# A language-model tower on one core: items of the front pipeline moved by a unit

## The reference

```python
logits = flat_x @ router_w + router_b
top_vals, top_idx = jax.lax.top_k(logits, K)      # K = 2 of E = 8 experts
rw = jax.nn.softmax(top_vals, axis=1)
def step(carry, xt):
    h, c = carry
    gates = xt @ Wi + h @ Wh + b
    i_, f_, g_, o_ = jnp.split(gates, 4, axis=-1)
    c = jax.nn.sigmoid(f_) * c + jax.nn.sigmoid(i_) * jnp.tanh(g_)
    h = jax.nn.sigmoid(o_) * jnp.tanh(c)
    return ((h, c), h @ Wo + bo)
```

## Time and profile before

| | us |
|---|---|
| median of three runs | 1628.14 |
| lowest and highest | 1626.41, 1628.58 |
| the profiled execution's own time | 1628.72 |
| its span, first to last instruction | 1626.9 |
| busy: TensorE, VectorE, ScalarE, POOL | 1549.8, 1491.1, 859.5, 58.1 |
| prologue, until step 0's first tanh | 101.4 |
| step 0 | 51.9 |
| a steady step (559.0 to 660.1) | 101.1 |
| step 14, step 15 | 93.8, 63.8 |

### The profile page before, as it was taken

The page is one execution under the profiler, slowest core; times in us unless marked ns, Lnnn a source line. Parts: engine busy times, 40 slices in busy tenths (PEclk is TensorE's granted clock), DMA queues, the critical chain, the costliest instruction groups (busy, mean ns, idle before and its releaser), DMA issues.

```text
span 1626.9 us, 21424 instructions
## 1 busy us (share of the span) xinstructions
PE 1549.8 (95%) x7325; PEld 742.2 (46%) x7325; DVE 1491.1 (92%) x2442; ACT 859.5 (53%) x1022; POOL 58.1 (4%) x47
## 2 busy tenths in 40 slices
PE   7778999999999999999999999999999999999998
PEld 3433444444444444454444444444444444444543
DVE  4777999999999999999999999999999999999986
ACT  4445455455554555555565464654646546465554
POOL 1000000000000000000000000000000000000000
PEclk8989999999999999999999999999999999999999
DMA  3325435444454543645435454464544535445453
GB/s 94 88 57 151 144 116 153 148 126 145 118 160 136 128 143 123 157 139 139 137 126 146 139 140 139 124 146 135 144 136 128 151 125 153 130 130 149 125 148 90
DMA packets 252545, 215.65 MB, mean 133 GB/s; under 512 B 131175, under 2 KB 174147, under 8 KB 252437
## 3 DMA queue, kind: packets, MB, share of 16 engines
q1 hardware_dynamic: 252356, 214.27, 46.9%
q10 hardware_dynamic: 80, 0.02, 0.0%
HBM read 73.17 MB, written 4.74 MB: 48 GB/s over the span
## 4 chain that ended last, share of the span: by engine, by line
DVE 61%; issue 16%; PE 13%; ACT 6%; POOL 2%; DMA 1%; SPq 1%; DVEq 0%; ACTq 0%
DVE H L1169 8%; DVE tmp L1202 8%; DVE C L1176 6%; DVE C L1206 5%; DVE tmp L1194 5%; DVE xm L1161 4%; PE gates L653 3%; PE gates L650 3%; DVE H L1184 3%; DVE z L1215 2%; POOL rstd L1301 2%; PE gates L655 2%; DVE xn L968 1%; DVE stats L935 1%; PE yp L661 1%
## 5 line engine op out<-in xcount | busy, mean ns | idle before, releaser
L819 ACT ACTIVATE tmp<-gates,bias_sb 128x1024 f32<-128x1024 f32 (+1 forms) x504 | 533.7, 1062 | 407.5 <-PE gates L655 373.3
L653 PE MATMUL gates<-H,wh_sb 128*128 128x512 f32 x960 | 491.9, 594 | 0.0
L655 PE MATMUL gates<-H,wh_sb 128*128 128x512 f32 x896 | 458.5, 593 | 0.0
L650 PE MATMUL gates<-xm,wi_sb 128*128 128x512 f16 x1512 | 413.3, 383 | 22.9 <-ACT tmp L819 17.4
L650 PEld LDWEIGHTS gates<-xm,wi_sb 128*128 128x128 f16 x1512 | 142.1, 99 | 315.9 <-issue 192.6
L655 PEld LDWEIGHTS gates<-H,wh_sb 128*128 128x128 f32 x896 | 170.8, 191 | 215.4 <-issue 215.4
L826 ACT ACTIVATE tmp<-C 128x1024 f32<-128x1024 f32 (+1 forms) x128 | 128.5, 1004 | 253.4 <-DVE C L1206 246.8
L653 PEld LDWEIGHTS gates<-H,wh_sb 128*128 128x128 f32 x960 | 182.9, 191 | 69.5 <-issue 0.5
L1194 DVE SCALAR_TENSOR_TENSOR tmp<-tmp 128x1024 f32<-128x1024 f32 (+1 forms) x120 | 140.8, 1174 | 17.9 <-ACT tmp L819 17.9
L1176 DVE COPY_PREDICATED C<-masks,Cx 128x1024 f32<-128x1024 uint16 (+1 forms) x120 | 154.3, 1286 | 0.0
L1184 DVE SCALAR_TENSOR_TENSOR H<-tmp 128x1024 f32<-128x1024 f32 (+1 forms) x128 | 147.7, 1154 | 5.3 <-ACT tmp L826 4.9
(11 more groups left out here) (286 smaller groups left out, 1238.8 us busy)
## 6 DMA issues: line engine op xcount, KB each, us to landing
Hx<-H SPq DMA_DIRECT2D x232, 256.0 KB, 2.9
Cx<-C SPq DMA_DIRECT2D x232, 256.0 KB, 2.4
masks<-mask_scratch SPq DMA_DIRECT2D x128, 256.0 KB, 5.1
roww<-mw_scratch SPq DMA_DIRECT2D x128, 256.0 KB, 3.4
diag<-pr SPq DMA_DIRECT2D x60, 112.0 KB, 3.5
diag<-vwin SPq DMA_DIRECT2D x60, 112.0 KB, 3.2
out_dram<-h SPq DMA_DIRECT2D x16, 256.0 KB, 2.6
C<-in_wi SPq DMA_DIRECT2D x1, 2048.0 KB, 10.8
```

Source lines behind the costliest of these rows:

```text
L650: last = mm(fed, wi_sb[:, e, wpart, rows_of], xm[:, e % 2, vpart, :], start=(wpart == HI and vpart == HI), stop=(first and wpart == LO))
L653: last = mm(fed, wh_sb[:, e, rows_of], H[:, e, 0:SEQ], start=False, stop=True)
L655: last = mm(other, wh_sb[:, e, rows_of], H[:, e, SEQ:2 * SEQ], start=True, stop=True)
L819: A(tmp[:, gate_at(gate, e), 0:width(s)], gates[:, (n - 1) % 2, 0:width(s)], ACT.Tanh, bias=bias_sb[:, e, gate:gate + 1], scale=UNSCALE).t ...
```

## The change

Items move in the four tables; nothing is computed differently. ScalarE's copies after `qkv` are cut into `q` (unit 27) and `kv` (unit 28), and `split` goes to unit 29. `moments` goes from unit 23 to 22 and the embedding's items from 22 to 21. `pw` goes behind `q_lo`, `kv_lo` from unit 29 to 30; `v_win`, `summary`, `window`, the feature part, `proj`, `projT`, `x2T`, `moments2`, `xn2`, `choice` and `weights` go one unit on, `f_part` two. `add_y` goes from unit 7 to 6, in front of the cell. `EARLY` becomes 17. In step 0 `chosen` stands a unit sooner, ahead of the input part.

```diff
-    SP_AT = dict(ids=-16, qbd=-3, vz=1, rows=25, wrow=28)
-    PE_AT = dict(emb=-10, xT=-6, qkv=-5, summary=-2, window=0, feature=6, values=12, proj=15, projT=16, x2T=19,
+    SP_AT = dict(ids=-17, qbd=-2, vz=1, rows=25, wrow=28)
+    PE_AT = dict(emb=-11, xT=-6, qkv=-5, summary=-1, window=1, feature=7, values=12, proj=16, projT=17, x2T=20,
                  logits=21, maskT=25)
-    ACT_AT = dict(h=-10, xT=-6, qkv=-5, split=-4, summary=0, window=3, pr_hi=7, feature=8, proj=15, x2T=19,
-                  choice=21, maskT=25)
-    DVE_AT = dict(onehot=-14, moments=-9, xn=-8, pw=-4, q_lo=-4, kv_lo=-3, v_win=-2, w_max=-1, s_max=1, s_sub=2, w_sum=3,
-                  w_out=4, s_sum=5, s_norm=6, f_max=7, p_lo=8, p_T=9, f_sum=10, f_part=10, attn=13,
-                  moments2=16, xn2=17, x_lo=20, choice1=21, choice2=21, weights=22)
-    EARLY = 16
+    ACT_AT = dict(h=-11, xT=-6, q=-5, kv=-4, split=-3, summary=0, window=4, pr_hi=8, feature=9, proj=16, x2T=20,
+                  choice=22, maskT=25)
+    DVE_AT = dict(onehot=-15, moments=-10, xn=-8, pw=-3, q_lo=-4, kv_lo=-2, v_win=-1, w_max=0, s_max=2, s_sub=3, w_sum=4,
+                  w_out=5, s_sum=6, s_norm=7, f_max=8, p_lo=9, p_T=10, f_sum=11, f_part=12, attn=13,
+                  moments2=17, xn2=18, x_lo=21, choice1=22, choice2=22, weights=23)
+    EARLY = 17
...
-    YT_AT, YBACK_AT, YADD_AT = 5, 6, 7
+    YT_AT, YBACK_AT, YADD_AT = 5, 6, 6
...
-                if t == ACT_AT["qkv"]:
+                if t == ACT_AT["q"]:
...
                     last.then_inc(S["qhi"], 1)
+                if t == ACT_AT["kv"]:
                     act.wait_ge(S["kp"], b1)
...
-                    if t == YADD_AT and not first:
-                        add_y(s - 1, 1 - par)
...
-                    if g == 2 and e:
+                    if first and g == 1 and e:
                         chosen(s, e - 1)
-                    elif g == 2 and not first:
+                    if g == 2 and e and not first:
+                        chosen(s, e - 1)
+                    elif g == 2 and not e and not first:
                         chosen(s - 1, E - 1)
                     run_front(lambda u, b: front(u, b, b % 2), t, s)
                     if g == 1:
                         input_part(s, e, first)
+                    if t == YADD_AT and not first:
+                        add_y(s - 1, 1 - par)
                     if g == 2 and not first:
                         cell(s, e)
```

## The result

The change makes the kernel slower: 1653.32 us median (1649.02 to 1653.85) against 1628.14 (1625.42 to 1628.58), a ratio of 1.0146 [1.0135, 1.0158]. Forecast were 1622.5 us and 1611 to 1636. The profiled execution took 1653.85 us, its span is 1652.1, 25.2 us over that of before.

| us | before | after | difference | forecast |
|---|---|---|---|---|
| prologue | 101.4 | 106.4 | +5.0 | |
| step 0 | 52.0 | 55.8 | +3.8 | both together -0.5 |
| steps 1 to 13 | 1315.9 | 1332.4 | +16.5 | -5.2 |
| steps 14, 15 | 157.7 | 157.4 | -0.2 | 0 |

The account below looks back on a forecast made before the run. It took a once-per-step loop through nearly full VectorE and TensorE as the bound: 0.40 us less per step, -5.2 over 13, and -0.5 in prologue and step 0, gave 1622.5 us, range 1611 to 1636.

Parts of the forecast that it names:

- piece A: VectorE alone, from unit 29's input part to the start of swap_c at unit 27: 93.36 us before, 93.67 forecast after.
- Rival (5): POOL's power beside the cell holds VectorE up, 1.9 - 0.4 us per step, 1642 us in all; chance 0.03.
- TensorE's waits "cost nothing": New waits at values (0.1 us), y of unit 16 (0.5) and projT (0.9) cost nothing; VectorE has over 0.8 in hand.
- piece B: Rest of the step's loop, swap_c of unit 27 to unit 29's input part: 7.69 us before, 6.98 forecast, decided by TensorE.
- one batch of the prologue: One batch of 13 idle matmuls (2.97 us) goes; clock effect taken as 0, at the other end +3 us.
- the block copies: First operand blocks (qbd), issued by SP at unit 30: about 6 us needed, over 11 available, so no cost.
- The gain of moments: Moments a unit sooner: VectorE's 0.90 us wait for POOL's power ahead of xn leaves each step.
- the price of kv_lo: kv_lo moves to unit 30 and adds 1.21 us per step to VectorE's own stretch of the loop.
- the relief of ScalarE: The split copies move behind tanh 29, taking 1.06 us per step out of ScalarE's stretch of the loop.
- no wait at unit 1, unit 2 or for masks: Input part 1 and cell 2 taken at nothing (ends 0 and 0.5 us per step); masks with 1 us to spare.
- y_bias free: add_y ahead of cell frees y_bias of its 0.5 us wait and delays cell by 0.6, neither in the loop.
- Rival (3): Gain replaced: 0.4 us per step at input part 1 or cell 2, or prologue's 3.5 not returned; 1628 us, chance 0.20.

## Why the prediction was wrong, point by point

The forecast's span was 1626.9 - 5.7 = 1621.2 us, the measured one is 1652.1: 30.9 us too few. The runs split them (differences of spans by stage):

| us | |
|---|---|
| steps 1 to 13 without low clock: 1315.2 by the run with idle matmuls, forecast 1310.7 | +4.5 |
| low clock in them: 1332.4 - 1315.2 | +17.2 |
| prologue and step 0: 162.2, forecast 152.9 | +9.3 |
| steps 14 and 15 | -0.2 |

**The step that failed** is one sentence: the other moves "(summary, window and feature parts one unit on, f_part two, moments2, xn2, choice and weights one) stay inside A and change only its order, at nothing, if each input is in time". xn2's input was not in time. The prediction priced the first norm's power at 1.92 us and took the second's, behind moments2, as unchanged (1.39 us before). But that duration depends on what VectorE runs when the power starts. moments2 went to unit 17, and the one-hot rows came to the same unit from 18. The diff shows it in `onehot=-15`, and neither the list of moved items nor the prediction names it. The price is read from the run with the input part first, whose units are all those of the changed kernel: piece A is 93.1 us there and 94.1 here (steps with full clock), 1.0 us per step. That the forecast's 93.67 is only 0.4 off is luck: without the wait piece A is 0.55 us shorter than the forecast's sum, and no run isolates what saves that.

**Rival (5) had the right two engines and the wrong loser.** It let POOL hold VectorE up beside the cell, and that did not come: L1203 and L1207 took 1.22 and 1.23 us beside the power. VectorE held POOL up, at the other power. The text even used "no more than elsewhere" on VectorE's row alone; that POOL's own power took 1.92 us there and 1.39 at the other norm of the same trace was not asked after. The Trainium skill's "SBUF — State Buffer" (two separate sides) says of the shared ports that the later one fully blocks until the first has finished. The prediction found the trace against this page because hidden kept its 1.23 us. But hidden (635.31) had started ahead of the power (635.48), so by the page's rule POOL is the one to wait. For POOL the traces agree where VectorE's instruction, with two inputs in SBUF, is already running. The power takes 1.01 us beside an idle VectorE, and 1.39, 1.91 and 1.92 where an instruction ends 0.5 or 1.0 us after its start, each over about 0.9 us after that end. The page's rule does not give 2.9 or 4.7 us, through several instructions. Nor does it give that VectorE goes on at once with its next instruction at its usual duration, as swap_h does in before (612.93, 1.30 us) beside the rest of the power.

**TensorE's waits "cost nothing"** was the second failed step, and the dearest. In the loop alone it is right: with full clock piece B is 6.96 us against 6.98 forecast, with maskT waiting 0.30 (forecast 0.5) and projT 0.72 (0.9). But the wait of 1.30 us at the logits, which the prediction did not work out, has half clock behind it in eight of the twelve steps 2 to 13, and with it piece B of 8.2 to 8.6 us and in three steps a cell at unit 22 that waits over 1 us. With that wait filled by idle matmuls the half clock is gone and 17.2 us with it. The Trainium skill's "TensorE: Matmul & The Clock Gate" (Part 1) has half clock after idling; the forecast weighed it for one batch of the prologue only. The traces agree in that half clock follows a wait, but not every wait brings it.

**Prologue and step 0.** The forecast said for the block copies "go out at unit 30, need about 6 us and have over 11", which holds in the steps. In the prologue the same unit stands behind wh's load on SP. It was not looked at: 12.2 us, 6.0 of them in the prologue and 6.2 behind it in step 0. Without it the two would have been 2.9 us shorter than the forecast's 152.9, within its 4. The 12.2 us are not wh's alone, though: with the norm back, the other order of SP gave 6.3 (batch included), and with wh's load where it is, the norm back or the one-hot rows back shortened step 0 by 5.4 and 4.4 us. The causes share part of step 0. The idle matmuls that were lost are 11 and not 13: the table's entry of 13 took the place of the 11 at unit 21, and unit 22 has none (7314 matmuls in all against 7325).

**What held.** The gain of moments, 0.90 forecast and 0.86 measured per step (11.2 us over steps 1 to 13); the price of kv_lo and the relief of ScalarE, alone 1.31 (94.74 less a mean of 93.43 before) and 1.05 against 1.21 and 1.06; waits ahead of q_lo, pw and the input part at 0.81, 0.42 and 1.23 in the undisturbed step (0.9, 0.5, about 1); no wait at unit 1, unit 2 or for masks; y_bias free. Rival (3), the gain replaced by a stall, came true in the steps with full clock (101.0 us, as before), at a place that it did not name.

**Open:** why the clock falls behind the logits in some steps and not in others of the same waits, and why it holds with the norm back, where TensorE waits 0.8 and 1.4 us 14 to 20 us ahead of the logits. Shown is only that with the logits' idle time filled no step from 1 to 14 has it. Why step 0 follows wh's load was not tried.

## What to carry to other kernels

Try the parts of a change one at a time: here the embedding's items and moments, moved by themselves, were worth all of the gain (0.9930), and the other parts that were tried nothing or less. Before moving an item, look at the other engine's small instruction that it hands work to: what stands right behind the hand-over is part of the move, and if that is an instruction on few partitions (16 here), put a wide one ahead of it. And where a matrix engine is 95% busy, a stall of a microsecond in its order need not be free, even where its consumer has slack: fill it in one run and read the granted clock.

## What the runs showed of the hardware that was not expected

- POOL's power on 128x4 values takes 1.01 us when VectorE is idle, and otherwise mostly ends about 0.9 us after an end on VectorE. If the VectorE instruction at its start works on 128 partitions, it is that one's end (power 1.11 to 1.92 us). A reduction with one input on 128 partitions did not hold it at all: 1.01 us beside L1034, in the prologue of the run with moments alone. If the VectorE instruction at the power's start works on 16 partitions, POOL gets in at no later boundary between two instructions, not even between wide ones, but only when VectorE has nothing to run: 2.84 to 4.71 us in full steps, in seven kernels, whether the narrow one is a comparison or a copy, with one or two inputs, on float32 or int32.
- In the other direction nothing was held up: VectorE's instructions keep their durations beside the power (1.22, 1.23 and 1.30 us on 128x1024).
- Four block-copy issues of 112 KB each on SP take 2.99 us ahead of a 2 MB load and 8.80 us right behind it.
